# A fused decoder kernel on one core: in the third stage's attention, two of four head groups get their exponentials straight from PSUM, with the maximum as a bias per head

## What is computed

```python
def _L1_xattn_ref(x, y, pad_mask, Wq, Wkv):
    q = (x @ Wq.T).reshape(B, N, H, d).transpose(0, 2, 1, 3)
    ...
    attn = jnp.einsum('bhnd,bhmd->bhnm', q * scale, k)
    attn = jnp.where(pad_mask[:, None, :, None], attn, jnp.float32(-1000000000.0))
    attn = jax.nn.softmax(attn, axis=-1)
    out = jnp.einsum('bhnm,bhmd->bhnd', attn, v)
    return out.transpose(0, 2, 1, 3).reshape(B, N, C)
```

## Time and profile before

| | us |
|---|---|
| median of three runs | 2672.06 (2667.97 to 2676.70) |
| the profiled execution | 2680.18 |
| span of that execution, first to last instruction | 2677.7 |
| share of the span that PE is busy | 87% |
| DVE, ACT | 60%, 61% |
| a round of the third stage, where nothing disturbs it | 103.85 |

### The profile page before, as it was taken

How to read it: one execution, slowest core, us unless ns; L and a number is a source line. 1 busy time by engine, 2 the same in 40 slices (tenths; PEclk the granted TensorE clock), 3 DMA queues, 4 the chain that set the end, 5 groups by cost and what they waited for, 6 DMA issues and landing times.

```text
span 2677.7 us, 93035 instructions
## 1 busy us (share of the span) xinstructions
PE 2339.2 (87%) x41378; PEld 1733.9 (65%) x41378; DVE 1615.5 (60%) x3692; ACT 1622.6 (61%) x3788; POOL 295.4 (11%) x396
## 2 busy tenths in 40 slices
PE   3888888888888559999999999999999999999997
PEld 2666566666666337767667677676676676776765
DVE  3666766676667555655665655555555656565564
ACT  2767666766676335656656656656566566566663
POOL 0001110111010001011001001100110011011100
PEclk8999999999999779999999999999999999999998
DMA  3000000000000100000000000000000000000000
GB/s 110 8 9 7 10 8 9 9 8 8 9 9 8 31 25 7 6 8 7 7 9 7 7 8 7 7 7 6 9 7 7 9 6 7 8 7 6 8 6 4
DMA packets 55338, 29.76 MB, mean 11 GB/s; under 512 B 24225, under 2 KB 53217, under 8 KB 54945
## 3 DMA queue, kind: packets, MB, share of 16 engines
q1 hardware_dynamic: 50624, 21.90, 3.0%
q10 hardware_dynamic: 4320, 1.97, 0.3%
HBM read 18.60 MB, written 5.24 MB: 9 GB/s over the span
## 4 chain that ended last, share of the span: by engine, by line
PE 38%; DVE 13%; ACT 11%; issue 2%; DMA 0%; SPq 0%; DVEq 0%
PE bank L1120 5%; PE bank L1187 2%; PE bank L1317 2%; ACT PT L1372 2%; DVE h L1520 2%; DVE zels L451 2%; ACT zels L1372 2%; DVE m L449 2%; PE bank L1250 2%; PE bank L1150 1%; PE bank L356 1%; PE bank L1310 1%; DVE h L1633 1%; PE bank L1160 1%; ACT zels L1392 1%
## 5 line engine op out<-in xcount | busy, mean ns | idle before, releaser
L1030 POOL TENSOR_TENSOR PT<-zels,unit 128x512 f32<-128x512 f32 x160 | 203.7, 1273 | 1469.5 <-ACT zels L1372 1282.0
L356 PE MATMUL bank<-w_gate,ident 128*128 128x128 f32 (+3 forms) x1024 | 316.0, 397 | 14.4 <-DVE mx L876 14.4
L425 ACT ACTIVATE zels<-zels 128x512 f32<-128x512 f32 x384 | 237.8, 632 | 105.4 <-DVE zels L451 105.0
L451 DVE TENSOR_TENSOR zels<-bank,m 128x512 f32<-128x512 f32 x384 | 265.6, 692 | 13.3
L449 DVE TENSOR_REDUCE m<-bank 128x4 f32<-128x512 f32 x384 | 262.1, 683 | 18.2 <-PE bank L370 10.4
L391 PE MATMUL bank<-ident,zels 128*128 128x128 f32 x1536 | 223.0, 282 | 17.7 <-ACT zels L425 13.2
L1372 ACT ACTIVATE zels<-bank 128x512 f32<-128x512 f32 (+1 forms) x256 | 142.6, 573 | 151.8 <-PE bank L1219 76.1
L391 PEld LDWEIGHTS bank<-ident,zels 128*128 128x128 f32 x1536 | 170.9, 143 | 54.8 <-ACT zels L425 38.6
L1372 ACT ACTIVATE PT<-bank 128x512 f32<-128x512 f32 x256 | 148.0, 598 | 92.5 <-PE bank L1293 50.4
L428 ACT ACTIVATE PT<-bank 128x512 f32<-128x512 f32 x384 | 202.3, 597 | 2.4 <-PE bank L391 2.3
L356 PEld LDWEIGHTS bank<-w_gate,ident 128*128 128x128 f32 x1024 | 159.8, 194 | 57.6 <-issue 33.7
(11 more groups left out here) (292 smaller groups left out, 5025.2 us busy)
## 6 DMA issues: line engine op xcount, KB each, us to landing
ctxT<-in_ctxT_dram SPq DMA_DIRECT2D x64, 48.0 KB, 1.8
x_after_cross_attention<-x SPq DMA_DIRECT2D x32, 64.0 KB, 1.5
h<-x_after_cross_attention SPq DMA_DIRECT2D x8, 256.0 KB, 2.8
xin<-x_after_cross_attention SPq DMA_DIRECT2D x32, 64.0 KB, 1.8
out_dram<-xn SPq DMA_DIRECT2D x32, 64.0 KB, 1.6
x<-in_xT_dram ACTq DMA_DIRECT2D x30, 64.0 KB, 1.8
input_integers<-xq SPq DMA_DIRECT2D x8, 128.0 KB, 2.0
xq<-input_integers SPq DMA_DIRECT2D x32, 32.0 KB, 1.8
```

The source lines that it names most:

```text
L356: mm(bank[:, 0:cols], ident[:, :], w_gate[:, :, :].rearrange("p a b -> p (a b)")[:, 0:cols], start=True, stop=True)
L425: act.activation(n.zels[:, u, :], n.zels[:, u, :], ACT.Exp, scale=ATT_SCALE).then_inc(ph.act[s], ph.AC.step(s, f"{t}P{u}"))
L451: dve.tensor_tensor(n.zels[:, u, :].rearrange("p (h k) -> p h k", h=HU), scores, top.unsqueeze(2).broadcast_to([P, HU, P]), ALU.subtract). ...
L1030: pool.tensor_tensor(n.TI[:, k % 2, :, :], (n.PT0, n.PT1)[k % 2][:, :, 1, :], unit[:, :].unsqueeze(1).broadcast_to([P, NP, DK]), ALU.add)\
```

## The change

In the third stage alone, and there for groups 0 and 2 (`FROM_PSUM`), DVE no longer writes `less`. ACT waits for `max` in place of `less`, reads the scores in PSUM, and takes the exponential head by head, four instructions of 128 columns, each with its head's column of `m` as the bias. For that to have the right sign, the query is made with the factor -8^-0.5 (a `scalar_tensor_tensor` in place of a `tensor_tensor`), the maximum becomes a minimum, and the scale of the exponentials is -1. Groups 1 and 3 are as before but for the signs. The lane orders and the amount of fill are the same.

```diff
-    dve = [f"{a}Kbd", *[x for u in units for x in (f"{a}max{u}", f"{a}less{u}")], f"{a}inv", f"{a}out"]
+    less = [f"{a}less{u}" for u in units if a != "y" or u not in FROM_PSUM]
+    dve = [f"{a}Kbd", *[x for u in units for x in (f"{a}max{u}", f"{a}less{u}") if "max" in x or x in less], f"{a}inv", f"{a}out"]
...
+FROM_PSUM = (0, 2)
...
-                    if warm["P"]:
+                    if t != "y" and warm["P"]:
...
-                if stage == f"{t}S{u}":
+                if stage == f"{t}S{u}" and t == "y" and u in FROM_PSUM:
+                    act.wait_ge(ph.dve[s], ph.DV.upto(it, f"{t}max{u}"))
+                    for j in range(HU):
+                        cols = slice(j * P, (j + 1) * P)
+                        last = act.activation(n.zels[:, u, cols], b[u][:, cols], ACT.Exp, scale=-1.0, bias=n.m[:, HU * u + j:HU * u + j + 1])
+                    last.then_inc(ph.act[s], ph.AC.step(s, f"{t}P{u}"))
+                elif stage == f"{t}S{u}":
                     act.wait_ge(ph.dve[s], ph.DV.upto(it, f"{t}less{u}"))
-                    act.activation(n.zels[:, u, :], n.zels[:, u, :], ACT.Exp, scale=ATT_SCALE).then_inc(ph.act[s], ph.AC.step(s, f"{t}P{u}"))
+                    act.activation(n.zels[:, u, :], n.zels[:, u, :], ACT.Exp, scale=-1.0 if t == "y" else ATT_SCALE)\
+                        .then_inc(ph.act[s], ph.AC.step(s, f"{t}P{u}"))
...
-                dve.tensor_tensor(n.qT[:, :], b[0][:, 0:P], n.qmask[:, :], ALU.mult).then_inc(ph.dve[s], ph.DV.step(s, "yq"))
+                dve.scalar_tensor_tensor(n.qT[:, :], b[0][:, 0:P], -ATT_SCALE, n.qmask[:, :], ALU.mult, ALU.mult).then_inc(ph.dve[s], ph.DV.step(s, "yq"))
...
-                    dve.tensor_reduce(top, scores, AX_X, ALU.max).then_inc(ph.dve[s], ph.DV.step(s, f"{t}max{u}"))
+                    dve.tensor_reduce(top, scores, AX_X, ALU.min if t == "y" else ALU.max).then_inc(ph.dve[s], ph.DV.step(s, f"{t}max{u}"))
+                    if t == "y" and u in FROM_PSUM:
+                        continue
```

More of the change, by code:

```diff
@@ L1010, in decoder @@
                  "lna": 1, "lnav": 0, "lngv": 1, "lny": 0, "lnyv": 0, "lnf": 0, "lnfv": 1,
-                 "y": {"S": 0, "P": 0, "OT": 0, "AT": 0}}
+                 "y": {"S": 0, "OT": 0, "AT": 0}}
         halves = ((0, DK), (DK, P))
```

## The result

| | before | after |
|---|---|---|
| median, us | 2670.41 (2667.97 to 2677.30, six runs) | 2657.28 (2655.77 to 2660.63, six runs) |
| span of the profiled execution | 2677.7 | 2654.2 |
| a round where nothing disturbs it | 103.85 | 103.15 |

The changed kernel takes 0.9948 of the time before, with a 95% interval of 0.9933 to 0.9963: 13.1 us less by the medians, where 8.2 had been forecast. The two profiled executions are 23.5 us apart and overstate this; the one of before is a long one, with a round of 110.13 us at a granted clock of 0.97, and the one of after is the second fastest of its six. Two runs far off all others, one of the kernel before (7173.1) and one of after_quarter (4287.9), are in no time given here.

A forecast was written before the change was run, and what follows sets the result against it. PE was taken to bound the kernel, with DVE in the chain only at lane 0's attention; 8.5 + 1.4 - 1.7 = 8.2 us gained, so 2672.06 - 8.2 = 2663.9 us, range 2655 to 2676.

The forecast's parts named there:

- PE's supply: PE, running with fewer pauses, reaches its instruction stalls sooner; a fifth of 8.5 us, 1.7, taken off the gain.
- Pitch: New 128-column exponentials on ACT: 0.257 us each, 1.03 a group, 0.51 more than before; far bound 0.343.
- Place A: Lane 0's attention, where the chain runs through DVE: the last exponential earlier, 0.77 us gained a round.
- The walk: Instruction-by-instruction timing of lane 0's attention on DVE, ACT and PE: last exponential at 1565.75 in place of 1566.53.
- Place B: Lane 1's attention: 0.51 us more on ACT, covered by 0.37 and 0.17 before the sum of squares; cost 0.0.
- The last attention: Program's end, no other lane beside it, ACT waiting for DVE before each exponential: 1.4 us gained, once.
- How many rounds: Third stage: 11 of 16 rounds counted as gaining 0.77 us, 8.5 in all; the others 0.0 to 0.2.
- Slower exponentials: Rival: a group on ACT takes 1.37 us, lane 1's attention costs 0.31 a round; 3.2 us slower, 2675; chance 0.12.
- The clock rival: Rival: earlier PE supply stalls grow longer and the clock falls in three more rounds; 11 us slower, 2683; chance 0.10.
- Supply eating a part: Rival: instruction supply, or a pitch between the bounds, eats part of the gain; 0 to 6 us gained; chance 0.30.
- Busy time: Whole profile: DVE's busy time falls by some 44 us (64 x 0.69), ACT's rises by some 33 (64 x 0.51).
- the chances: Odds for the measured time: faster 0.45 (0.36 and 0.10), slower by over 0.3% 0.12, within 0.3% 0.43.

The follow-up runs named there:

- after_quarter: Changed kernel plus 16 matmuls of 16 columns in the setup, moving PE's later instructions: median 2666.35 us, against 2675.11 for the kernel before with the same matmuls.
- one_exponential: Changed kernel, but groups 0 and 2 take one exponential of 512 columns without subtracting the maximum: ratio 0.9945 to the kernel before, 12.2 us less.
- lane0_only: Changed kernel with the change kept in lane 0 alone, lane 1 keeping all four subtractions: ratio 0.9963 to the kernel before, 8.6 us less.
- lane1_only: Changed kernel with the change kept in lane 1 alone, lane 0 keeping all four subtractions: ratio 1.0005 to the kernel before, 3.3 us more.
- shifted pair: Kernel before and changed kernel, each with 32 matmuls of 16 columns added ahead of the third stage: 2687.17 and 2683.93 us, 3.2 apart.
- three pairs: Before and changed kernels with PE's instructions unmoved, with 16 matmuls added in the setup, or 32 ahead of the third stage: changed 13.1, 8.8, 3.2 us less.
- two_columns: Changed kernel, but the new exponentials' scale is a column of -1 instead of an immediate: ratio 1.0008 to the kernel before, 3.4 us more.

## Why the prediction was right, and where it was off

The direction, the place and the mechanism were right, and the time lies in the range; the size was 8.2 for 13.1. That it came so near is in part luck: see PE's supply below.

- **Pitch.** 0.257 was taken, 0.25 to 0.26 measured. Line 579 was the right row, though its column is a scale and not a bias. The Trainium skill, "ScalarE: Activation LUTs", section "What ACT_TABLE_LOAD costs", makes 0.387 for the duration, and the trace agrees (a mean of 0.386 after); with its overlap of 0.093 the pitch would be 0.294, an estimate that is 0.04 too high, as the overlap in the trace is 0.13.

```profile
L429 ACT ACTIVATE zels<-bank,m 128x128 f32<-128x128 f32 x256 | 73.8, 386 | 27.8 <-DVE m L458 27.8
```

- **Place A.** The walk gave the first copy at 3.20 after the query (measured 3.20), the second at 5.74 (5.72), the last `less` at 7.06 (7.04), the last exponential at 7.90 (7.79 to 7.84), the gain 0.77 (0.80 at the transposes of the output). Its parts hold alone as well: 0.19 for group 0, 0.73 for group 2. That ACT and DVE set the start of the last exponential together is shown by one_exponential. Two steps of the walk were wrong and did no harm. The start moved by 0.89 and not by 0.78, and 0.09 of that is lost again, as the last exponential and the copies last longer. And PE did not bring the last four transposes forward by 0.77: they start some 8.98 after the query (the second half of the row below) where it was 9.36, so by 0.38. The product behind them waits for ACT's copies, so it is ACT alone that gives the 0.80.

```profile
1564.00 1.09 PE L393 MATMUL bank<-ident,zels 128*128 128x128 f32 x8
```

- **Place B.** This step was wrong: cost 0.0, measured 0.13. I counted 0.17 us between the end of the last square and the sum of squares as cover. It was next to none: after, the square is late and the sum still starts 0.15 after its end (1605.12 + 1.08 to 1606.35). So of the 0.17 all but 0.02 passes between the two engines in any case. The other part of the cover, 0.37, was right, and 0.51 - 0.37 = 0.14 is the cost. With this an undisturbed round is 0.77 - 0.14 = 0.63 shorter; measured 0.70.
- **The last attention.** 1.4 was forecast. In the profiled pair its last exponential starts 5.89 us after the query in place of 6.99, and the transposes of the output 9.66 in place of 11.37, so 1.7. Part of this is the clock, which stood at half for 8.9 us of that stretch before and 6.8 after; between lane0_only and lane1_only, with 6.8 in both, the same difference is 1.0, and in the shifted pair, with 6.8 in both, 1.2. From there to the end another 3.0 us are gone in the profiled pair, and these are the clock's: in all fourteen traces the stretch from the start of the last transposes of the output to the end of the last engine's work goes by how long the clock stood at half in it: 12.7 us with 0.8 to 1.3 us, 13.5 to 13.7 with 4.2 to 4.6, 14.4 with 8, 15.4 to 15.6 with 12. For the stretch from 2660 to 2665 before it was at half, in the like one after at full.

```profile
2660.00:2665.00 5.00, 3.55 (x10) 2.33 (x11) 0.84 (x3) 0.61 (x2) 0.00 (x0) 0.50 0.00 0
```

```profile
2640.00:2645.00 5.00, 3.31 (x16) 1.92 (x15) 1.13 (x4) 0.96 (x3) 0.00 (x0) 1.00 0.00 0
```

- **How many rounds, and PE's supply.** This is the term that was mis-sized. I took 11 rounds of 16 and a fifth off. Eleven is what place A shows, but the others gain in part too, and the sum without disturbances is 16 x 0.70 = 11.2 and 1.0 to 1.7 at the end, some 12.5, next to the measured 13.1: by the medians, supply took nothing on balance at this position of the instructions. In the profiled pair it even gave, as one round of 110.13 at a lower clock is gone. That is not a constant. At the other two positions the change brought some 4 and 9 us less than this sum. The forecast's 8.2 is near the mean of the three pairs (8.4), which three draws do not prove.
- **The rivals.** "Slower exponentials" did not occur; two_columns made it happen and gave +3.4 where the forecast had +3.2 for it, though by other parts: place B cost 0.48 a round and not 0.31. The clock rival did not occur here. Supply eating a part, given 0.30, is what the shifted pairs show.
- **Busy time.** DVE's fell by 44.2 us (1615.5 to 1571.3) where 44 was forecast, ACT's rose by 26.0 (1622.6 to 1648.6) where 33 was. Why ACT's rose by less is open. In the chances, 0.36 and 0.10 make 0.46 and not 0.45, on which nothing hangs.

What stays open is why a given timing meets more or fewer supply stalls and falls of the clock. The runs show that the instruction at which PE stands can be the same in two kernels and that moving the list changes which rounds are disturbed. What a stall costs and what the fall of the clock behind it costs is not told apart: of the 26 stalls of 1.2 us or more between 1034 and 2620 us in the fourteen traces, 14 had a fall to half the clock within 5 us of their start and 12 had none, among them one of 2.13 us in the kernel before.

## What to carry to other kernels

Walk one steady round through the engines' lists with measured pitches: here this gave the start of an instruction to 0.1 us in kernels not yet built, and it told apart two equal savings worth 0.19 and 0.73, because behind one stood an instruction that had to wait anyway. Time from the end of a producer to the start of its consumer on another engine is cover only beyond what is left when the consumer waits for nothing else, 0.15 us from ACT to PE here. Follow ends and not starts: at the same start and the same pitch ACT's instructions ended 0.10 us later behind the new exponentials, and PE waits for ends. And judge an edit of half a per cent by the undisturbed round as well as by the time: with a dense PE, the same edit gave 3, 9 or 13 us by where its instructions lay, so a small gain in the median can be a gain in position.

## What the runs showed that was not expected

- The position of PE's instructions alone moves the time: 16 tiny matmuls in the setup, hidden under a wait of 5.9 us, made the kernel before 4.4 us slower by the medians (2675.11 against 2670.74; ratio 1.0014, 1.0004 to 1.0023), with undisturbed rounds unchanged (103.81).
- A second column operand costs ACT 0.09 us in pitch, 0.34 against 0.25 (mean durations 0.473 and 0.386), which is enough to take this change's whole gain.
- Behind the last transposes of the output the clock makes the end of the program anything from 12.7 to 15.6 us long. In the profiled pair that is 3.0 us, more than the edit gained in the last attention.
- Each wait of 0.5 us or more of PE for its instructions, but for one place, ends 1.0 to 1.8 us after a packet of 16384 bytes of its instruction queue has landed.
